# Moving a norm's roots behind another multiply on GpSimd, and its normalisation from VectorE to ScalarE, in a fused recurrence and local-attention kernel

## The reference, cut to what matters

```python
def _layer(x, wqkv, qs, ksc, wo, lg, lb, w1, b1, w2, b2):
    h = shift_token(x)
    q, k, v = jnp.split(h @ wqkv, 3, axis=-1)
    ...
    q = l2norm(q) * qs
    k = l2norm(k) * ksc
    q, k = rotary_xpos(q, k)
    o = local_attention(q, k, v)
    x = x + o @ wo
    h = shift_token(x)
    mu = h.mean(-1, keepdims=True)
    var = h.var(-1, keepdims=True)
    h = (h - mu) / jnp.sqrt(var + 1e-05) * lg + lb
    h = h @ w1 + b1
    a, g = jnp.split(h, 2, axis=-1)
    h = a * jax.nn.gelu(g, approximate=False)
    return x + h @ w2 + b2
```

## Time and profile before

| | |
|---|---|
| median of 3 runs | 468.07 us (467.18 to 468.27) |
| the profiled execution | 469.18 us |
| its span, first to last instruction | 467.4 us |
| granted TensorE clock, mean | 0.916 of full |
| PE busy | 360.6 us, 77% |
| DVE busy | 329.4 us, 70% |
| POOL busy | 298.1 us, 64% |
| ACT busy | 284.6 us, 61% |

### The profile page before, as it was taken

How to read it: one execution, slowest core, us unless ns; L and a number is a source line. 1 busy time by engine, 2 the same in 40 slices (tenths; PEclk the granted TensorE clock), 3 DMA queues, 4 the chain that set the end, 5 groups by cost and what they waited for, 6 DMA issues and landing times.

```text
span 467.4 us, 11257 instructions
## 1 busy us (share of the span) xinstructions
PE 360.6 (77%) x3832; PEld 296.1 (63%) x3832; DVE 329.4 (70%) x744; ACT 284.6 (61%) x852; POOL 298.1 (64%) x247
## 2 busy tenths in 40 slices
PE   1574066899998999899899989988949895778372
PEld 1353045777776878687678868876838674756242
DVE  6879963768778768868868787688766865743423
ACT  2362164768767868678777867777736672674020
POOL 2200439899999699969967994999467948620202
PEclk9996575999999999999999999999979999797857
DMA  8600131411431052124204310521114201300100
GB/s 278 172 0 0 39 113 31 126 30 30 112 78 29 12 147 51 28 65 116 49 11 131 78 35 1 147 64 31 29 39 113 56 0 28 74 2 1 23 22 22
DMA packets 42398, 28.21 MB, mean 60 GB/s; under 512 B 21699, under 2 KB 36597, under 8 KB 42357
## 3 DMA queue, kind: packets, MB, share of 16 engines
q1 hardware_dynamic: 42357, 27.68, 22.8%
HBM read 13.51 MB, written 3.15 MB: 36 GB/s over the span
## 4 chain that ended last, share of the span: by engine, by line
PE 44%; DVE 21%; POOL 12%; issue 10%; ACT 7%; DMA 2%; SPq 2%; DVEq 0%; POOLq 0%; ACTq 0%
PE bank L680 5%; PE bank L548 5%; PE bank L715 5%; PE bank L552 5%; POOL rn L483 4%; DVE h L1081 4%; PE bank L549 4%; DVE rot_sin L1057 3%; PE upper L664 3%; PE upper L643 3%; PE upper L637 2%; DVE rot_cos L1057 2%; PE bank L608 2%; POOL rot L519 2%; PE upper L615 2%
## 5 line engine op out<-in xcount | busy, mean ns | idle before, releaser
L831 ACT ACTIVATE probs<-upper,neg_max 128x128 f32<-128x128 f32 x256 | 90.4, 368 | 61.9 <-DVE neg_max L1103 61.8
L483 POOL TENSOR_TENSOR rn<-floored,minus_half 128x16 f32<-128x16 f32 x32 | 93.7, 2930 | 2.7
L504 POOL TENSOR_TENSOR rot<-rot_cos,rot_sin 128x512 f32<-128x512 f32 x32 | 40.9, 1278 | 61.2 <-DVE rot_sin L1057 34.4
L1103 DVE TENSOR_REDUCE neg_max<-upper 128x4 f32<-128x512 f32 x64 | 43.1, 683 | 32.7 <-PE upper L664 32.7
L519 POOL TENSOR_TENSOR rot<-rot,rn 128x1024 f32<-128x1024 f32 x32 | 60.9, 1903 | 1.9
L548 PE MATMUL bank<-wqkv_hi,act_t_hi 128*128 128x512 f32 x96 | 44.3, 461 | 21.4 <-DVE o_tok L1115 13.5
L831 ACT ACTIVATION_READ_ACCUMULATOR probs<-upper,neg_max 128x1 f32 x256 | 52.8, 206 | 0.0
L1057 DVE TENSOR_TENSOR rot_cos<-bank,tab 128x512 f32<-128x512 f32 x64 | 43.6, 682 | 2.4 <-PE bank L552 2.3
L1057 DVE TENSOR_TENSOR rot_sin<-bank,tab 128x512 f32<-128x512 f32 x64 | 43.5, 680 | 0.0
L1064 DVE TENSOR_REDUCE ss<-sq 128x16 f32<-128x1024 f32 x32 | 38.8, 1212 | 5.5 <-ACT sq L852 5.4
L548 PEld LDWEIGHTS bank<-wqkv_hi,act_t_hi 128*128 128x128 f32 x96 | 19.0, 198 | 36.2 <-issue 23.5
(11 more groups left out here) (129 smaller groups left out, 884.2 us busy)
## 6 DMA issues: line engine op xcount, KB each, us to landing
v_mid<-v_tok SPq DMA_DIRECT2D x64, 128.0 KB, 2.3
tab_raw<-tables SPq DMA_DIRECT2D x8, 512.0 KB, 3.5
h_tok<-group_in SPq DMA_DIRECT2D x14, 128.0 KB, 3.5
x_res<-group_in SPq DMA_DIRECT2D x28, 64.0 KB, 1.8
wqkv_raw<-wqkv SPq DMA_DIRECT2D x2, 768.0 KB, 6.5
x_in<-x SPq DMA_DIRECT2D x4, 256.0 KB, 4.5
head_scale<-head_scales SPq DMA_DIRECT2D x8, 128.0 KB, 4.0
group_in<-normed SPq DMA_DIRECT2D x4, 256.0 KB
```

The costliest lines, as they stand in the source:

```text
L483: pool.tensor_tensor(rn[:, 0:2 * HEADS], floored[:, 0:2 * HEADS], minus_half[:, :], ALU.pow).then_inc(rn_ready, 1)
L831: last = act.activation(probs[:, h, :], s_bank[half][:, (h % 4) * P:(h % 4 + 1) * P], ACT.Exp, bias=neg_max[a.par][:, h:h + 1], accum_out= ...
L1103: dve.tensor_reduce(neg_max[a.par][:, 4 * half:4 * half + 4], src, AX.X, ALU.max, negate=True).then_inc(max_ready, 1)
```

## The change

POOL no longer takes the four inverse deviations between the 16 roots of the step and the multiply by them, but behind that multiply. It takes the mean times -1 before (L526) and the product of this and the inverse deviation after (L530 of the new file), so that the norm can be written as h * scale + bias. ACT then normalises, with four activations of Identity that have a scale and a bias for each partition, ahead of its copies `q_t` and `k_t`; the four instructions of DVE are gone.

```diff
@@ POOL's body
                     if cur.valid:
                         norm_roots(t)
-                    if j == 1 and not (number and G < 1):
-                        deviation_roots(G, h2_var, h2_floored, h2_dev)
                     if j == 3 and (G > GROUPS if number else layer == DEPTH - 1):
                         deviation_roots(G - GROUPS, y_var, y_floored, y_dev)
                     if cur.valid:
...
                                            ALU.mult).then_inc(rot_scaled, 1)
+                    if j == 1 and not (number and G < 1):
+                        pool.wait_ge(h2_var, G)
+                        need(pool, h2_ready, G - 1)
+                        settle(pool)
+                        pool.tensor_scalar(h2_mean[:, :], mean_var[:, 0:GT, 0], -1.0, None, ALU.mult).then_inc(h2_means, 1)
+                        deviation_roots(G, h2_var, h2_floored, h2_root)
+                        pool.wait_ge(h2_root, G)
+                        pool.wait_ge(h2_means, G)
+                        pool.tensor_tensor(h2_shift[:, :], h2_mean[:, :], rn[:, 2 * HEADS:], ALU.mult).then_inc(h2_dev, 1)
                     if not number and layer == 0 and j == 2:
                         low_half(G)
@@ ACT's body, behind the copy of probs_t, ahead of q_t and k_t
+                    if j == 2 and not (number and G < 1):
+                        act.wait_ge(h2_dev, G)
+                        for k in range(GT):
+                            last = act.activation(h2[:, k, :], h2[:, k, :], ACT.Identity, bias=h2_shift[:, k:k + 1],
+                                                  scale=rn[:, 2 * HEADS + k:2 * HEADS + k + 1])
+                        last.then_inc(h2_ready, 1)
                     if prev.valid:
                         act.wait_ge(qt_done, prev.t + 1)
@@ DVE's body
                     if mid.valid and j != 1:
                         save_probs(mid)
-                    if ffn:
-                        normalise_tiles(h2, h2, h2_dev, G).then_inc(h2_ready, 1)
                     if cur.valid:
                         sum_squares(cur)
```

More of the change, by code:

```diff
@@ L154, in sandwich_kernel @@
         h2_t = sb("h2_t", [P, GTOK])
+        h2_mean, h2_shift = sb("h2_mean", [P, GT]), sb("h2_shift", [P, GT])
         h2_hi, h2_lo = sb("h2_hi", [P, GTOK], F32R), sb("h2_lo", [P, GTOK], F32R)
@@ L220, in sandwich_kernel @@
         y_normed = sem("y_normed")
+        h2_means, h2_root = sem("h2_means"), sem("h2_root")
         dve_chain = sem("dve_chain")
```

## The result

| | before | changed |
|---|---|---|
| median of 20 executions each | 468.00 us | 472.24 us |
| fastest and slowest | 465.51 to 470.98 | 468.98 to 479.26 |
| ratio of the times, 20 and 17 executions | | 1.0089, 95% interval 1.0066 to 1.0112 |
| the profiled execution | 469.18 us | 476.34 us |
| its span | 467.4 us | 474.5 us |

The change made the kernel slower by 4.2 us, or 0.9%. Two things stand out: the fastest execution moved by 3.5 us, and the spread of the executions grew from 5.5 to 10.3 us. The profiled execution of the changed kernel is one of its three slowest, which the ratio leaves out, so it is read here for distances between instructions and not for the total.

What follows compares the result with a forecast made beforehand. No engine alone was taken as the bound: each step is a chain across engines. 0.30 + 5 x 0.25 + 0 + 0.95 = 2.5 us slower gave 471.7 for the profiled execution, 470.6 for the median; range 466.0 to 473.0.

Steps and rivals of the forecast that it cites:

- The removed rows end when POOL pauses, and are mostly waiting: VectorE's four h2 rows, body 3: 3.1 us read as 1.1 us work and 2 us waiting for POOL.
- The new last thing is `k_t`: Step 2, bodies 1 to 6: PE's h2 transposes would wait for ScalarE's copy k_t, ending at 235.45 in body 3.
- 0.30 and 0.25 us for each of the six bodies: Later start of PE's h2 transposes: 0.30 us in body 3, 0.25 each in bodies 1, 2, 4, 5, 6.
- the upper end for the mean row and for the hand-overs: Mean row 0.25 us and two hand-overs 0.14: 0.23 us more in each six bodies and the last; 472.2 us.
- 0.95 us for body 8: Body 8, all in series: h2 transposes at 447.35 in place of 446.41, 0.95 us later.
- Body 7 costs nothing: Body 7: ScalarE's four end at 420.8, PE comes to h2 only at 422.14, so no cost.
- Rival C: PE's clock falls behind the joined pause in step 2: 3.6 us in each of six bodies, about 494 us; 4%.
- Rival A: Waiting for POOL simply gone: at most 1.45 us gained in each of six bodies, less 0.95, 460.3 us; 12%.
- Rival B: Norm's inputs ready by 232.26, no hold by POOL: 1.6 us gained, 0.95 lost in body 8, 467.4 us; 22%.

Runs made afterwards that it cites:

- e1: The changed kernel run again, with no edit; 475.6 us against 467.4 for the kernel before.
- e10: The changed kernel with body 8 as before, VectorE normalising there without mean and shift rows; 474.2 us against 468.4 for the kernel before.
- e3: Kernel before with roots behind the multiply, VectorE normalising, and POOL waiting for h2_ready before its step 2 additions; 461.0 us against 467.4.
- e5: Kernel before with only POOL's wait for h2_ready ahead of its step 2 additions; 464.6 us against 468.3.
- e2: Kernel before with only POOL's roots moved behind the multiply, VectorE normalising, no mean and shift rows; 478.1 us against 467.4.
- e9: The version of e3 measured again on another chip; 460.2 us against 468.4 for the kernel before.
- e6: The changed kernel with POOL's four short rows ahead of the step 1 multiply; 470.9 us against 468.3 for the kernel before.
- e4: The changed kernel with ScalarE's four activations behind its copies q_t and k_t; 466.1 us against 467.4 for the kernel before.

## Why the prediction was right, point by point

The median of 472.24 us lies in the range of 466 to 473, and the change is slower, as forecast. The mechanism was right too: `k_t` became the last thing, and its shift and body 8 are 3.8 of the 4.2 us. The forecast of 470.6 was 1.6 us short. That the median is inside the range owes something to luck: the range had no term for the clock, and e1 and e10, the changed kernel again and with body 8 as before, gave 475.6 and 474.2 on other chips.

- *The removed rows end when POOL pauses, and are mostly waiting.* Right, shown by e3 and e5; e2 adds that each of them waits for a row of POOL of its own. The Trainium skill, "SBUF — State Buffer", section "SBUF: two separate sides", describes one pair of ports that GpSimd and some VectorE instructions take exclusively, for a whole instruction, with ScalarE outside of it. The runs agree: VectorE's each take 0.33 to 0.40 us with POOL still and 1.3 beside an addition of POOL, and ScalarE's four, beside POOL's additions in six bodies and with POOL idle in two, follow each other at 0.39 us as in the earlier trace rows, with no long one among the 32:

```profile
L872 ACT ACTIVATE h<-h,h_shift,rn x32: 477/479/521, 144.9 to 453.1; 128x128 f32<-128x128 f32 x32
```

- *The new last thing is `k_t`.* Right: all six waits of PE for h2 end with L882, after 1.94 or 1.95 us.
- *0.30 and 0.25 us for each of the six bodies.* The sign and the place were right, the size was 0.48 and 0.43. All of the 0.18 lies in POOL's short rows: the first starts 0.09 us behind the end of the multiply and not 0.03 ahead of it (it stands behind three added waits, which the text had put at nothing; that they are the reason was not tried), the mean row took 0.24 and the power 1.04. On the way to PE, ScalarE started 0.03 behind the shift and PE 0.10 behind `k_t`, both put at 0.05, and ScalarE's copies took 0.03 less: together nothing. The text had the upper end for the mean row and for the hand-overs, 0.23 us more; what came, 0.18 more, is near that end.
- *0.95 us for body 8.* It was 1.16: the first short row starts 0.22 us behind the variances (before 0.08), and the four activations take 1.65. Bodies 1 to 6 and 8 make 3.8 in place of the 2.5 forecast.
- *Body 7 costs nothing.* Right at its place: PE has no wait for h2 there, and the distance is 16.41 us where it was 16.42.
- *Rival C, the clock falls, 4%, at 3.6 us a body.* This is the step that was farthest off. The mechanism is real: behind the joined pause the clock was at the lower level for a while in four of six bodies of one execution and in two of another. But the lower level holds for only a part of the feed-forward (the stretches above), and costs 0.9 us a body. It should have been a part of the forecast with a price per hit of 1 us, not a rival with all six bodies at once. At 0.9 us a hit, six places can give 0 to 5.4 us by execution; that lengthens only the upper side, which the range of 466 to 473 did not have: 8 of the 20 executions are above 473. The rival's time doesn't add up either: 470.6 and 6 x 3.6 are 492, not 494.
- *Rival A, 460.3 us if only the waiting were gone.* For the changed kernel it did not come, by the sum of ScalarE's rows as argued. e3 and e9, which take the wait away and leave the work on VectorE, are at 461.0 and 460.2. That this is so near A's price is chance: it is another sum, of 9.5 us by the distances less 3.3 in e9, with nothing lost in body 8 and body 7 by execution.
- *Rival B.* Its condition did not come: the shift was there 0.68 us behind ScalarE's last copy, where the forecast had 0.51. In e6 the inputs come in time, but by another way, with the short rows ahead of the multiply; there the change is slower all the same, since what moves these rows up moves PE's transposes down. B as it stood, with shorter rows in their place, was not tried.

## What to carry to other kernels

Before moving an instruction to another engine, ask of what its duration consists. Rows that each end with a row of another engine, and take three times their time without it, are waiting; here it was cheaper to hold that other engine for a microsecond than to move the rows. Then ask what the held engine's rows will stand beside: in e3 they slowed two other rows of VectorE. Where several things release one instruction, lay all of them beside each other for each version; here PE, the copy of k and h2 were ready within 1.1 us of each other in body 3 (234.87, 234.03, 235.06), and single edits made each of them the last in turn. And add to a joined pause of PE the price of a clock that may fall behind it: some idle transposes in the pause show about how much it is.

## What the runs showed of the hardware that was not expected

- Pauses of PE of the same length, at the same place of the program, are followed by a fall of the granted clock in one body and not in the next, and in other bodies in the next execution. Behind a pause of 1.95 us the clock fell in four, two and (e10) three of six bodies, behind 2.28 us (e2) in two of six, and behind 1.19 us (e4) in none of six. Behind the pause of 1.85 us at another place (e6) it fell in none of six either, so the length alone does not tell.
- VectorE's 128x128 rows with POOL at work take not a fixed time but that of the row of POOL beside them: 1.29 to 1.33 us beside an addition of 1.25 to 1.31, 0.76 beside a row of 0.72, and 0.33 to 0.40 with POOL still. Not every row of POOL does this: in body 3 of the kernel before, `h_lo` (L1119, from 237.35) took 0.69 us beside the power L483 (236.71 to 239.64), as long as with POOL idle in body 7.
- e3 and e9 have executions of 464 to 466 us beside those of 459 to 460, with mean clocks of 0.897 to 0.908. The clock is 1.00 behind the h2 transposes of their bodies 1 to 6. The kept traces, e3's of 465.11 us and e9's of 460.25, tell where it fell. Two stretches of e3 around its body 7, and the same of e9:

```profile
405.00:409.00 4.00, 3.64 (x20) 3.42 (x22) 0.27 (x4) 2.59 (x7) 1.21 (x2) 0.57 0.01 4
415.00:419.00 4.00, 4.00 (x43) 3.53 (x44) 1.72 (x5) 1.01 (x2) 0.00 (x0) 0.57 0.02 4
...
405.00:409.00 4.00, 4.00 (x84) 3.52 (x83) 0.12 (x1) 2.05 (x4) 0.83 (x1) 1.00 0.01 4
415.00:419.00 4.00, 2.47 (x18) 1.60 (x14) 1.50 (x4) 2.73 (x3) 0.00 (x0) 1.00 0.02 4
```

From the last 16 roots to the h2 transposes of body 7 it is 18.60 us in e3 and 15.71 in e9, and from there to those of body 8 24.03 and 22.25: 4.7 of the 4.9 us between the two spans. The kernel before has 16.42 and 24.27, so its own profiled execution paid 2.7 us there, and e9's 8.2 us over it are in part this place. What decides it from one execution to the next stays open.
